# Attention of the experts: the weighted sums of two key tiles issued together in every second step, and the maxima turned through a full-width TensorE matmul padded with zeros

## The reference

```
# E=4 experts, B=4 sequences of 512 tokens, NH=16 heads of DH=16
q, k, v = heads(h @ aiw + aib)
attn = softmax(q @ k.T * SCALE)          # 512 x 512 for every head
o = attn @ v                             # 512 x 16 for every head
h = o @ aow + aob
# then zx = h @ wi + b for both directions, which the LSTM reads
```

## Time and profile before

| what | us |
|---|---|
| median of 3 runs | 5326.97 (5326.27 to 5326.97) |
| the profiled execution | 5325.8 |
| its span, which all rows below count from | 5324.0 |
| first score of the stage, last one | 643.24, 1943.6 |
| PE busy over the span | 5025.1 (94%) |
| DVE busy over the span | 4120.1 (77%) |
| ACT busy over the span | 2395.4 (45%) |

### The profile page before, as it was taken

The page is one execution under the profiler, slowest core; times in us unless marked ns, Lnnn a source line. Parts: engine busy times, 40 slices in busy tenths (PEclk is TensorE's granted clock), DMA queues, the critical chain, the costliest instruction groups (busy, mean ns, idle before and its releaser), DMA issues. The chain is left out here.

```text
span 5324.0 us, 258931 instructions
## 1 busy us (share of the span) xinstructions
PE 5025.1 (94%) x108704; PEld 3528.2 (66%) x108704; DVE 4120.1 (77%) x19249; ACT 2395.4 (45%) x8347; POOL 1150.2 (22%) x5133
## 2 busy tenths in 40 slices
PE   7978799999999996999999999999999999989895
PEld 4654433333333335999999999999999999974442
DVE  3855666666666658999999999999999999972225
ACT  2633465555555544444444444444444444433332
POOL 0000011111111101333333333333333333320000
PEclk9988899999999998999999999999999999999997
DMA  0023544545544441101111011110111011111200
GB/s 15 1 87 120 152 68 92 126 86 103 109 92 107 90 139 64 40 19 38 40 24 40 16 40 32 33 40 16 40 24 40 25 31 40 24 52 44 72 32 12
DMA packets 378774, 302.09 MB, mean 57 GB/s; under 512 B 146105, under 2 KB 357561, under 8 KB 372954
## 3 DMA queue, kind: packets, MB, share of 16 engines
q1 hardware_dynamic: 378382, 298.20, 23.4%
HBM read 179.14 MB, written 119.01 MB: 56 GB/s over the span
## 5 line engine op out<-in xcount | busy, mean ns | idle before, releaser
L1437 PE MATMUL bank<-lparts,lstate 128*32 128x256 bf16 x98304 | 2696.6, 273 | 55.1 <-PEq L1380 46.7
L1437 PEld LDWEIGHTS bank<-lparts,lstate 128*32 128x32 bf16 x98304 | 2461.6, 97 | 290.6 <-issue 47.5
L1448 DVE STREAM_TRANSPOSE ltz<-bank 128x256 f32<-128x256 f32 x2048 | 920.7, 450 | 8.3 <-PE bank L1437 3.8
L1512 ACT ACTIVATE ltc<-lgc 128x16 f32<-128x16 f32 x2049 | 443.1, 216 | 1030.0 <-DVE lgc L1469 1030.0
L1526 POOL TENSOR_TENSOR wh<-lgate,ltc 128x16 f32<-128x16 f32 x2052 | 471.6, 230 | 1798.3 <-ACT ltc L1512 1728.3
L1253 ACT ACTIVATE wh<-bank 128x512 f32<-128x512 f32 x1024 | 550.1, 600 | 482.9 <-PE bank L1040 482.3
L1165 DVE TENSOR_REDUCE bnegmax<-bank 128x1 f32<-128x512 f32 x1024 | 654.0, 682 | 130.7 <-PE bank L1022 130.4
L1507 ACT ACTIVATE lgate<-lz 128x48 f32<-128x48 f32 x2048 | 498.7, 244 | 520.8 <-DVE lz L1459 520.8
L1533 POOL COPY ltz<-wh 128x64 f32<-128x64 f32 x2048 | 603.2, 295 | 0.0
L1455 DVE TENSOR_TENSOR lhalf<-ltz 128x128 f32<-128x128 f32 x2048 | 582.1, 284 | 9.5 <-POOL ltz L1533 5.4
L1102 PE MATMUL bank<-xT,bw 128*128 128x512 f32 x1024 | 489.4, 602 | 2.7 <-DVE bzs L1186 1.9
(11 more groups left out here) (210 smaller groups left out, 4306.9 us busy)
## 6 DMA issues: line engine op xcount, KB each, us to landing
zx<-bzs SPq DMA_DIRECT2D x32, 2048.0 KB, 7.2
wh<-zx SPq DMA_DIRECT2D x64, 1024.0 KB, 7.5
qk<-eparts SPq DMA_DIRECT2D x96, 256.0 KB, 2.6
bqp<-qk SPq DMA_DIRECT2D x192, 128.0 KB, 4.8
bkp<-qk SPq DMA_DIRECT2D x192, 128.0 KB, 8.1
hs<-wh SPq DMA_DIRECT2D x32, 512.0 KB, 5.9
cmemT<-hs SPq DMA_DIRECT2D x32, 512.0 KB, 4.3
vx<-evx SPq DMA_DIRECT2D x16, 544.0 KB, 3.7
```

The costliest lines, as they stand in the source:

```text
L1437: last = nc.tensor.matmul(bank[x][32 * q:32 * q + 32, 0:256], top[:, x, e, k].rearrange("p m r -> p (m r)"), parts[:, way, g, k, n, e, q], ...
L1448: nc.vector.transpose(tz[:, x].rearrange("p (n w) -> p n w", w=SLOT)[:, :, 0:32], bank[x][:, 0:256].rearrange("p (n c) -> p n c", n=BLOCKS ...
L1512: nc.scalar.activation(tc[:, x], gc[:, x, 1], ACT.Tanh).then_inc(tanhed[x], 1)
```

## The change

Four edits. `values` is no longer called once in each step from 6 on: it is called twice in a row in each odd step from 7 on, for the two key tiles n = j-7 and n = j-6. The buffer `maxparts` has 99 columns for each query tile in place of 3; the parts stand in the last three of them and the other 96 are zeros. So `turn_maxima` writes rows 0 to 98 of bank 5 and no longer rows 96 to 98 alone. DVE sets the buffer to zero once, and PE and POOL wait for that before their loops.

```
-        maxparts = core.sb(ctx, "bmaxparts", [P, 2, BT, 3], BF16)
+        maxparts = core.sb(ctx, "bmaxparts", [P, 2, BT, KROWS + 3], BF16)
...
                     for qt in range(BT):
-                        last = nc.tensor.matmul(bank[5][KROWS:KROWS + 3, qt * P:(qt + 1) * P],
+                        last = nc.tensor.matmul(bank[5][0:KROWS + 3, qt * P:(qt + 1) * P],
                                                 maxparts[:, j % 2, qt], ident16[:], start=True, stop=True)
...
-                pe.wait_ge(zeroed, 3)
+                pe.wait_ge(zeroed, 4)
...
-                    if j >= 6:
-                        values((j - 6) // 4, (j - 6) % 4)
+                    if j >= 7 and j % 2 == 1:
+                        for n in (j - 7, j - 6):
+                            values(n // 4, n % 4)
...
                 nc.vector.memset(bank[6][:], 0.0).then_inc(zeroed, 1)
+                nc.vector.memset(maxparts[:], 0.0).then_inc(zeroed, 1)
...
-                    parts = [maxparts[:, j % 2, :, n] for n in range(3)]
+                    parts = [maxparts[:, j % 2, :, KROWS + n] for n in range(3)]
...
+                pool.wait_ge(zeroed, 4)
                 for j in range(HEADS):
                     split(j)
```

## The result

The changed kernel takes 5334.03 us (median of 20 runs, 5330.45 to 5337.12) against 5327.31 of the kernel before (20 runs, 5325.92 to 5333.43): the ratio is 1.0013, with a 95% interval of 1.0007 to 1.0019. That is 7 us slower, a small loss that lies within the 0.2% that were taken as the bound of no change. The forecast was 5339. Its sign holds, the size was too large by 5 us. Slower by over 0.2% had the largest chance, 0.53, and did not come; a result within 0.2% had 0.34. That the time lies in the range of 5320 to 5366 says little, since the range is 46 us wide and the change moved it by 7.

What follows compares the result with a forecast made beforehand. PE was taken to bound the stage, busy 199.98 of 200 us. Slabs 5.7, first slab 4.5, last steps 1.6 and clock 2 sum to 13.8, of which 12 were taken: 5327 + 12 = 5339, range 5320 to 5366.

Steps and rivals of the forecast that it cites:

- The rival in which PE's own time decides: All 128 pairs: each gets 0.27 us shorter, -34 us in all, to 5293; chance 0.13, part-ways too.
- forecast of 2.37: Odd steps with values twice: 2.37 us from score 3 to the next score, +0.82 or +0.88 on before.
- rival with up to 0.111: Wide turn's load not hidden: at 0.111 us a turn, 28 us more in odd and some 8 in even steps; chance 0.17.
- a pair with products (12 to 21): Five pairs in each of 15 slabs: odd step +0.82, even step -0.92 as bank 7 frees; -0.10 us a pair.
- steps 26 and 27: Second projection in the even step waits for ACT, starts 0.98 us earlier, against +0.88 in the odd: -0.10.
- steps 24 and 25: Step 24 gives back nothing, since DVE's maxima set the second next score; step 25 costs 0.88: +0.88 us.
- steps 22 and 23: Transpositions follow the turn and ACT's copy of the rows comes late for the next `score_t`: taken as +0.1 us.
- a slab: Steady part: 6 x -0.10 + 0.88 + 0.1 = +0.38 us a slab; 15 of them +5.7.
- a pair of the first slab: Steps 6 to 21, eight pairs: maxima and ACT's rows' copy hold PE; 7.1 us against 6.54, +0.56 each, +4.5 in all.
- clock, steps 0 to 5: Stage's start: clock rises with the values, now from step 7, so eight score passes run at 0.43 us: +2 taken.
- the last steps: Behind the last score: even steps give nearly nothing, odd steps cost 0.86 us; two pairs, +1.6.
- The 1.27 us "that left": Even step with two products: the time that left it, of which only 0.92 us are saved because of bank 7.

Runs made afterwards that it cites:

- fifth experiment: Changed kernel with the first product of an even step behind `score_t` 0, ahead of `score_t` 1 and 2: 5326.16 us against 5329.69 for the kernel before, ratio 0.9993.
- The fourth: Changed kernel, but up to step 21 the values one key tile in each step: 5329.15 us against 5326.33 for the kernel before, ratio 1.0005.
- the sixth: Changed kernel, but in steps 6 to 9 modulo 16 from 22 on the values one key tile at a time: 5329.22 us against 5329.69 before, ratio 0.9999.
- the second experiment: Kernel before with only the values of two key tiles together, the turn narrow as before: 5339.21 us against 5326.33, ratio 1.0024.
- the first: Kernel before with the wide turn alone, values of one key tile in every step as before: 5328.94 us against 5326.33, ratio 1.0006.
- the last experiment: Kernel before with the wide turn in steps 1 to 5 alone, narrow from step 6 on: one run, 5326.84 us against 5326.16.
- the eighth kernel: Changed kernel, values together only in steps 10 to 21 modulo 16 from 26, turn width by what follows, first product behind `score_t` 0: 5302.42 us against 5329.69 before.
- the third: Changed kernel with the first of an even step's two products behind scores 0 and 1, ahead of all three `score_t`: 5339.31 us against 5326.33 before, ratio 1.0024.

## Why the prediction was right, and where it wasn't

*The mechanism was right.* PE's pauses on the way into the strips and out of them are saved, and other engines take it back: bank 7 in the even steps with products, the maxima in steps 24, the maxima and ACT's copy of the rows in the first slab. The fifth experiment takes the wait for bank 7 away and gains 13 us where 16 were expected. The fourth and the sixth undo the change where the other waits stand, and get back 5.5 of 5.3 to 6 and 9 of 13. That it is the maxima and ACT which hold PE there is read from the traces, not tried apart. The rival in which PE's own time decides (-34 us) fell: it needed bank 7 and the maxima to be ready earlier. The Trainium skill, "TensorEngine Tiling (Array Packing)", section Key Properties, says that changing the tiling mode drains the engine. The trace agrees: with the narrow turn, as in the second experiment, score 3 and the turn start 0.31 apart, with the wide one 0.22. What it costs in time is set by what PE would have waited for otherwise.

*The wide turn costs nothing of its own: right.* 0.057 a turn, loads of 124 ns hidden. With values behind it the odd step is 0.035 longer, which the forecast of 2.37 had counted in. The rival with up to 0.111 fell. The figure of 81 ns of the Trainium skill, "TensorE: Matmul & The Clock Gate", section Back-to-back issue gap, does not hold for this stream; the trace has 57.

*The terms of the sum*, from the starts of scores in the two profiles:

| term | forecast | measured |
|---|---|---|
| a pair with products (12 to 21) | -0.10 | 11.285 - 11.37 = -0.085 |
| steps 26 and 27 | -0.10 | 11.18 - 11.54 = -0.36 |
| steps 24 and 25 | +0.88 | 8.61 - 7.72 = +0.89 |
| steps 22 and 23 | +0.1 | 8.00 - 7.94 = +0.06 |
| a slab | +0.38 | 84.21 - 84.02 = +0.19 |
| a pair of the first slab | +0.56 | 7.28 - 6.54 = +0.74 |
| clock, steps 0 to 5 | +2 | 19.6 - 22.1 = -2.5 |
| the last steps (from step 246 to the recurrence, with half a slab) | +1.6 | 164.2 - 161.8 = +2.4 |

Steps 6 to 21 make +5.3 (the first of the eight pairs only +0.09, since in the kernel before it was still partly at the low clock), fourteen slabs +2.6, the last steps +2.4, the clock -2.5: +7.8, and the recurrence starts 7.95 later. The profiled execution is 9.4 longer in all; the rest comes in stages that the change doesn't touch, and the medians say 6.7.

*The step that failed* is the clock: "They now begin in step 7, so eight score passes run at 0.43". It took the values as what lets the clock rise, because they began when it rose. No run shows that they do: in the second experiment the clock rose 0.34 us before them. The full-width turn brings the rise forward without any values, as the first and the last experiment show. The term has the wrong sign, 4.5 us between forecast and measurement.

The terms add up to 13.8, and the stage took 7.8 more. Of these 6.0 the clock is 4.5 and the steps 26 and 27 are 3.9; the other terms go the other way. The forecast took 12 for its 13.8 because the -0.10 of the pairs with products was uncertain. That pair came nearly as said, so it is luck that the 1.8 brought the forecast nearer. The 1.27 us "that left" in the even step has no working: from 1.48 to 0.44 behind score 3 is 1.04. No term uses it.

*Two terms were mis-sized.* In steps 26 and 27, "it starts at 906.81 in place of 907.79" came true for the second projection, counted from score 3: 0.50, in the changed kernel 910.85 against 910.35. What the -0.10 left out stands ahead of it. In the kernel before, the first projection of the step waits for ACT and starts 0.81 behind the first `score_t` (904.05 against 903.24) in place of 0.65, and its load is not hidden (the four instructions span 1.98 in place of 1.88). Both are gone in the changed kernel: 0.16 and 0.10, together the 0.26 between -0.10 and -0.36. This is PE's load queue in the kernel before:

```profile
903.03 0.53 PEld L1040 LDWEIGHTS bank<-bqp,bkp 99*128 99x128 bf16 x3
904.05 0.30 PEld L1087 LDWEIGHTS bank<-xT,bw 128*128 128x128 f32 x2 [0.49 <-ACT xT L1265]
```

and the projection in the changed kernel, which no longer waits (three `score_t` at 907.54, projection 0.65 later, the second 0.28 behind the turn):

```profile
907.54 0.81 PE L1040 MATMUL bank<-bqp,bkp 99*128 99x512 bf16 x3
908.19 1.88 PE L1087 MATMUL bank<-xT,bw 128*128 128x512 f32 x4
...
910.57 0.39 PE L1030 MATMUL bank<-bident,bmaxparts 128*99 128x128 bf16 x4
910.85 1.98 PE L1087 MATMUL bank<-xT,bw 128*128 128x512 f32 x4
```

With the values of two key tiles ahead of the last transpositions of step 25 ACT has caught up by then. In the sixth and the eighth kernel step 25 has the values of one key tile again, and step 10 modulo 16 is 0.23 and 0.27 longer. It is the same wait, as the trace of the sixth shows at that place:

```profile
909.47 0.30 PEld L1087 LDWEIGHTS bank<-xT,bw 128*128 128x128 f32 x2 [0.46 <-ACT xT L1271]
```

In the first slab "ACT starts the rows' copy at 2.8, done at 3.4" came 0.15 late: ACT goes on with exponentials until 2.92 and starts the copy at 2.95, so the next `score_t` starts at 3.59 of the pair in place of 3.44, and the few hundredths that are left between 7.1 and 7.28 lie behind it.

## What to carry to other kernels

Taking a pause out of the busiest engine is worth only the distance to the next thing that it waits for, so look up for each place which copy, maximum or exponential would be ready when, and regroup only where other work stands between; here that choice, with one product moved and the width of the turn chosen by what follows, gains 27 us where the same regrouping applied everywhere costs 7. When one wait is removed, look what was queued behind it before saying that the wait was not the cause: the third and the fifth experiment differ by one matmul's place. And what the change takes away in one step may have held up another engine in the next: look for waits ahead of the place that is counted.

## What the runs showed of the hardware

A full-width matmul whose columns are nearly all zeros (99 columns of weights, 96 of them zero) let TensorE's clock rise earlier from 1.2 to 2.4 GHz, under the same load of bf16 scores. With the 3-column turn PE worked from 643 to 669 us at the granted clock 0.50; with the 99-column one it was at 1.00 from 650 to 661 on. In the last experiment nothing else differs but the wider buffer, its memset and the wait for it. So of two matmuls of the same length one can bring the rise forward and the other not. What in it does that, the width, the rows of PSUM or the engine's mode, was not tried apart. The scores with the 3-column turn raise the clock too, only later: in the second experiment it rose at 672.9, before any values.

The other surprise is that columns of weights are cheap: 96 more of them lengthen the load by 40 ns, and the start of the next turn by 2 ns (57 against 55).
